# The first batch's quantisation spread over twenty items of cross attention and shared with GpSimd, its rows sent ahead of the down weights, and the first projections' waits split

## The reference

```python
x = layernorm(x + self_attention(x, W_K, W_Q, W_V, W_O))   # 16 heads of 128, causal
x = layernorm(x + gamma * cross_attention(x, ctx, ctx))    # 8 heads of 64, no projections
x = layernorm(x + ffn(x))

def ffn(x):                                    # hidden 2048
    xhat = (x - mean(x)) / sqrt(var(x) + 1e-8)
    s = 127 / max(abs(xhat))                   # for each token
    xq = clip(round(s * xhat), -128, 127) / s
    g = silu(xq @ sign(W_g).T)
    u = xq @ sign(W_u).T
    return (g * u) @ sign(W_d).T
```

## Time and profile before

| | us |
|---|---|
| median of 3 runs (lowest, highest) | 1461.12 (1459.65, 1461.98) |
| the profiled execution's own time | 1461.33 |
| its span, first to last instruction | 1459.5 |
| self attention, about | 0 to 985 |
| cross attention, about | 985 to 1212 |
| ffn, about | 1212 to 1459.5 |

### The profile page before, as it was taken

One profiled execution on the slowest core, in us unless ns is written; L12 is line 12 of the kernel. 1 busy time (PEld: TensorE's weight loads), 2 busy tenths in 40 slices (PEclk: granted clock), 3 DMA queues, 4 the chain that ended last, 5 costly groups with the idle time before them and its releaser, 6 DMA issues.

```text
span 1459.5 us, 23316 instructions
## 1 busy us (share of the span) xinstructions
PE 1416.3 (97%) x6912; PEld 1137.0 (78%) x6912; DVE 1086.8 (74%) x2346; ACT 713.3 (49%) x1528; POOL 624.9 (43%) x499
## 2 busy tenths in 40 slices
PE   7999999999999999999999999988999998999998
PEld 6788888888888888888888888867887774655665
DVE  4667676777777776767677777689989996698846
ACT  3444535354444444454545444547887873333333
POOL 1334434334253443443534425355655653344434
PEclk9999999999999999999999999999999999999999
DMA  6566666666666666666666666665556642101101
GB/s 182 150 181 180 190 162 181 169 185 177 174 174 184 167 175 180 180 190 162 185 175 180 179 175 183 197 171 151 131 142 164 185 124 95 37 1 65 37 29 58
DMA packets 210606, 219.33 MB, mean 150 GB/s; under 512 B 99712, under 2 KB 177536, under 8 KB 210560
## 3 DMA queue, kind: packets, MB, share of 16 engines
q1 hardware_dynamic: 209408, 218.24, 53.4%
q10 hardware_dynamic: 1152, 0.52, 0.2%
HBM read 128.98 MB, written 81.85 MB: 144 GB/s over the span
## 4 chain that ended last, share of the span: by engine, by line
PE 83%; DVE 9%; DMA 4%; ACT 2%; issue 1%; SPq 1%; POOL 1%; ACTq 0%; POOLq 0%; DVEq 0%
PE bank L517 35%; PE bank L555 11%; PE bank L524 8%; PE bank L542 8%; PE bank L1642 7%; PE bank L1630 6%; PE bank L1199 3%; PE bank L1153 2%; PE bank L1168 2%; DVE xneg_max L1303 1%; DVE xpT_lo L1310 1%; DMA xs<-rows_pair 1%; ACT xprobs L1241 1%; DVE acc L851 1%; DMA turned_scratch<-turned 1%
## 5 line engine op out<-in xcount | busy, mean ns | idle before, releaser
L662 ACT ACTIVATE probs<-probs,neg_max 128x128 f32<-128x128 f32 (+3 forms) x256 | 142.8, 559 | 356.9 <-DVE neg_max L791 349.6
L473 POOL TENSOR_TENSOR v_lo<-placed,v_hi 128x512 fp32r<-128x512 f32 x63 | 81.7, 1297 | 349.9 <-ACT v_hi L668 349.9
L475 POOL TENSOR_TENSOR pT_lo<-placed,pT_hi 128x1280 fp32r<-128x1280 f32 x63 | 186.3, 2957 | 0.0
L851 DVE SCALAR_TENSOR_TENSOR acc<-bank,prob_recip,acc 128x512 f32<-128x512 f32 x256 | 174.5, 745 | 4.9
L1598 POOL TENSOR_TENSOR prod_lo<-prod,prod_hi 128x512 fp32r<-128x512 f32 x64 | 85.1, 1329 | 137.3 <-ACT prod_hi L1680 137.3
L1092 POOL TENSOR_SCALAR xprobs<-xprobs,xprob_recip 128x512 f32<-128x512 f32 x128 | 87.3, 700 | 90.8 <-DVE xprob_recip L1314 90.8
L791 DVE CUSTOM_DVE_ANT_0 probs<-bank,mask 128x128 f32<-128x128 f32 (+3 forms) x256 | 117.2, 480 | 8.4
L766 DVE TENSOR_TENSOR qT_lo<-bank,qT_hi 128x512 fp32r<-128x512 f32 x64 | 44.2, 690 | 104.7 <-ACT qT_hi L650 104.7
L803 DVE STREAM_TRANSPOSE turned<-probs 128x256 f32<-128x256 f32 (+1 forms) x384 | 113.8, 361 | 0.0
L1642 PE MATMUL bank<-wdT_f32r,prod_hi 128*128 128x512 f32 x256 | 111.6, 436 | 0.8 <-POOL prod_lo L1598 0.6
L1241 ACT ACTIVATE xprobs<-bank,xneg_max 128x512 f32<-128x512 f32 x128 | 89.2, 697 | 42.3 <-DVE xneg_max L1303 40.6
(11 more groups left out here) (156 smaller groups left out, 3816.3 us busy)
## 6 DMA issues: line engine op xcount, KB each, us to landing
turned_scratch<-turned SPq DMA_DIRECT2D x64, 896.0 KB, 3.8
placed<-turned_scratch SPq DMA_DIRECT2D x252, 224.0 KB, 4.1
cp<-context_halves SPq DMA_DIRECT2D x64, 256.0 KB, 3.9
context_halves<-ctx_halves SPq DMA_DIRECT2D x16, 512.0 KB, 4.7
xs<-rows_pair SPq DMA_DIRECT2D x60, 128.0 KB, 3.7
acc<-in_x_dram SPq DMA_DIRECT2D x16, 256.0 KB, 4.4
rows<-in_L_attn_W_V_dram SPq DMA_DIRECT2D x64, 64.0 KB, 2.2
rows<-in_L_attn_W_O_dram SPq DMA_DIRECT2D x64, 64.0 KB, 2.7
```

The source lines that it names most:

```text
L475: nc.gpsimd.tensor_tensor(pT[par][1][:], landed_probs(landing), pT[par][0][:].bitcast(F32), ALU.subtract).then_inc(p_lo, 1)
L662: nc.scalar.activation(probs[:, cols], probs[:, cols], ACT.Exp, bias=low[:, par, t:t + 1], scale=-1.0, accum_out=total[:, par, t:t + 1]).t ...
L851: nc.vector.scalar_tensor_tensor(out=acc[:, b * NT + t, :], in0=s_bank[t][:], scalar=recip[:, b, t:t + 1], in1=acc[:, b * NT + t, :], op0= ...
```

## The change

Four things are edited. (1) In the first projections (batch 0) TensorE waits ahead of each of the three passes for what that pass reads, instead of ahead of the first for all; ScalarE copies wk after x3's cast, and VectorE turns wk ahead of x2 and wq after x3. (2) The quantisation of batch 0 runs beside items 9 to 28 of cross attention. VectorE keeps the statistics, the variances, the maxima, the steps and the turning. (3) Both norms' application and scaling with rounding become two GpSimd instructions for each of four tiles, with a wait between the two; they stand at the end of GpSimd's list of items 11 to 14, 17 to 20 and 23 to 26, the powers at the end of items 10 and 16. (4) SP sends and lands the turned rows ahead of all down weights, and `row_step` ahead of `xqT`.

```diff
...
         cross.begin_gpsimd(pool)
     def tensor(pe):
-        def project(name, b, bank, full):
+        def project(name, b, bank, full, first=False):
             w = wT[name]
             n = 0
             for wp, xp in SPLIT:
+                if first:
+                    pe.wait_ge((w_lo if wp else w_hi)[name], 1)
+                    pe.wait_ge(xt_lo if xp else xt_hi, NT)
                 for c in range(NC):
                     n += 1
                     last = nc.tensor.matmul(bank[:], w[wp][:, c * P:(c + 1) * P], xT[xp][:, c, b * S:(b + 1) * S],
...
                 scores()
             else:
                 full, free, bank = {"k": (k_full, k_lo, k_bank), "q": (q_full, q_lo, q_bank), "v": (v_full, v_turn, v_bank)}[what]
-                if n == 0:
-                    pe.wait_ge(w_lo["w" + what], 1)
-                else:
+                if n > 0:
                     pe.wait_ge(free, n)
-                pe.wait_ge(xt_lo, (n + 1) * NT)
-                project("w" + what, n, bank, full)
+                    pe.wait_ge(xt_lo, (n + 1) * NT)
+                project("w" + what, n, bank, full, n == 0)
         def step(h, b):
             i = h * B + b
...
         for name in BEGIN:
             what, n = name[0], int(name[1:])
             if what == "x":
-                if n == 2:
-                    weight_hi("wk", 1)
                 act.wait_ge(xt_full, n + 1)
                 nc.scalar.copy(xT[0][:, :, n * P:(n + 1) * P],
                                X_BANK[n][:].rearrange("p (c n) -> p c n", n=P)).then_inc(xt_hi, 1)
                 if n == 3:
+                    weight_hi("wk", 1)
                     weight_hi("wq", 1)
                 if n == 4:
                     weight_hi("wv", 1)
...
         for name in BEGIN:
             what, n = name[0], int(name[1:])
             if what == "x":
-                if n == 1:
+                if n == 2:
                     turn_weight("wk", 1)
-                if n == 3:
-                    turn_weight("wq", 1)
                 if n == 4:
                     turn_weight("wv", 1)
                 if n == 8:
...
                 cols = slice(n * P, (n + 1) * P)
                 nc.vector.tensor_tensor(xT[1][:, :, cols], X_BANK[n][:].rearrange("p (c n) -> p c n", n=P),
                                         xT[0][:, :, cols].bitcast(F32), ALU.subtract).then_inc(xt_lo, 1)
+                if n == 3:
+                    turn_weight("wq", 1)
             elif what == "k":
                 lo(kT, k_bank, k_hi, n + 1, k_lo)
             elif what == "q":
...
         return b + (h + d) // XH, (h + d) % XH
-    QUANT_FROM = B - 2
-    GAP = 2 * NT + 1
-    NQ_AT, AMAX_AT = GAP + NT, 2 * (GAP + NT)
-    LEVELS_AT = AMAX_AT + NT
-    SCALE_AT = LEVELS_AT + 1
-    ROUND_AT, TURN_AT = SCALE_AT + NT, SCALE_AT + 2 * NT
+    QUANT_FROM = XH + 1
+    N2_POW, N2_APPLY, NQ_STATS, NQ_POW, NQ_APPLY, AMAX, ROUNDED, TURN = 1, 2, 4, 7, 8, 10, 14, 18
     def exists(n, limit):
...
         pool.wait_ge(norm1.rstd_ready, 2)
     def gpsimd(pool):
+        def quantise_beside(pool, i):
+
+            if i == N2_POW:
+                norm_gpsimd(nc, pool, quant.norm2, k.minus_half, 0)
+            if 0 <= i - N2_APPLY < NT:
+                quant.apply_beside(pool, quant.norm2, quant.normed, 0, i - N2_APPLY)
+            if i == NQ_POW:
+                norm_gpsimd(nc, pool, quant.norm_q, k.minus_half, 0)
+            if 0 <= i - NQ_APPLY < NT:
+                quant.apply_beside(pool, quant.norm_q, quant.hat, 1, i - NQ_APPLY)
+            if 0 <= i - ROUNDED < NT:
+                quant.round_beside(pool, i - ROUNDED)
+
         def step(b, h):
             m = b * XH + h
             if h % 2 == 0 and exists(m + 4, ITEMS):
...
                 queries_lo(pool, nb, nh // 2)
             if is_item(b, h, 1, 1):
                 quant.clear_steps(pool)
-            if is_item(b, h, QUANT_FROM, 2):
-                norm_gpsimd(nc, pool, quant.norm2, k.minus_half, 0)
-            if is_item(b, h, QUANT_FROM, 6):
-                norm_gpsimd(nc, pool, quant.norm_q, k.minus_half, 0)
             if exists(m + 2, ITEMS):
                 normalise(pool, m + 2, (h + 2) % 4)
             if pair_ends(b, h):
...
             if normalises(b) and h == XH - 1:
                 norm_gpsimd(nc, pool, norm1, k.minus_half, b + 2)
                 pool.wait_ge(norm1.rstd_ready, b + 3)
+            quantise_beside(pool, m - QUANT_FROM)
         batches(pool, step)
...
                     norm1_stats(dve, b + 2, NORM1_STATS.index(u))
                 if u == NORM1_VAR:
                     norm_var(nc, dve, k, norm1, LN_EPS, b + 2)
-                return
-            v = (b - QUANT_FROM) * XH * NT + u
-            if v % NT == 2:
-                return
-            n = v // NT * (NT - 1) + min(v % NT, 2)
-            if n == 0:
+            quantise_beside(dve, b * XH + u // NT - QUANT_FROM, u % NT)
+
+        def quantise_beside(dve, i, j):
+
+            if i == 0 and j == 0:
                 dve.wait_ge(z_added, PAIRS + 1)
                 dve.wait_ge(signs.kept, H * 48 + 1)
                 dve.wait_ge(source.halves_kept, H * 16)
-            quantise_beside(dve, n)
-
-        def quantise_beside(dve, n):
-
-            for norm, at, eps, stage in ((quant.norm2, 0, LN_EPS, quant.normed), (quant.norm_q, NQ_AT, FFN_EPS, quant.hat)):
-                if 0 <= n - at < NT:
-                    quant.stats(dve, norm, 0, n - at)
-                if n - at == NT:
-                    norm_var(nc, dve, k, norm, eps, 0)
-                if 0 <= n - at - GAP < NT:
-                    quant.apply(dve, norm, stage, 0, n - at - GAP)
-            if 0 <= n - AMAX_AT < NT:
-                quant.tile_amax(dve, 0, n - AMAX_AT)
-            if n == LEVELS_AT:
+            if i == 0:
+                quant.stats(dve, quant.norm2, 0, j)
+            if i == N2_POW and j == 0:
+                norm_var(nc, dve, k, quant.norm2, LN_EPS, 0)
+            if 0 <= i - NQ_STATS < NT and j == 0:
+                quant.wait_beside(dve, quant.norm2.done, 0, i - NQ_STATS)
+                stats_tile(nc, dve, quant.norm_q, tile_of(0, i - NQ_STATS), i - NQ_STATS, 0)
+            if i == NQ_POW and j == 1:
+                norm_var(nc, dve, k, quant.norm_q, FFN_EPS, 0)
+            if 0 <= i - AMAX < NT and j == 0:
+                quant.wait_beside(dve, quant.norm_q.done, 1, i - AMAX)
+                quant.tile_amax(dve, 0, i - AMAX)
+            if i == AMAX + NT - 1 and j == 1:
                 quant.levels(dve, 0)
-            if 0 <= n - SCALE_AT < NT:
-                quant.scale_tile(dve, 0, n - SCALE_AT)
-            if 0 <= n - ROUND_AT < NT:
-                quant.round_tile(dve, 0, n - ROUND_AT)
-            if n == TURN_AT:
+            if 0 <= i - TURN < 2 and j % 2 == 1:
+                quant.turn_tile(dve, 0, 2 * (i - TURN) + j // 2)
+            if i == TURN and j == 0:
                 quant.turn_steps(dve, 0)
-            if 0 <= n - TURN_AT < NT:
-                quant.turn_tile(dve, 0, n - TURN_AT)
         def step(b, h):
             m = b * XH + h
...
         self.x_scratch = nc.dram_tensor("x_turned_scratch", (P, self.E, NC * NT * self.R), BF16).ap()
         self.step_scratch = nc.dram_tensor("steps_scratch", (P, self.R), F32).ap()
         self.cleared = sem("steps_cleared")
+        self.beside_half, self.beside_done = sem("quant_half_done"), sem("quant_tile_done")
         self.amax_ready, self.recip_done, self.per_unit_ready = sem("amax_ready"), sem("amax_recip_done"), sem("per_unit_ready")
         self.scaled_ready, self.xq_ready = sem("scaled_ready"), sem("xq_ready")
         self.x_turn, self.step_turn = sem("xq_turned"), sem("steps_turn_done")
...
     def apply(self, dve, norm, out, b, t):
         apply_tile(self.nc, dve, norm, self.normed(b, t), out(b, t), t, b)
+    def wait_beside(self, dve, done, stage, t):
+
+        if t == NT - 1:
+            dve.wait_ge(done, 1)
+        else:
+            dve.wait_ge(self.beside_done, stage * (NT - 1) + t + 1)
+
+    def apply_beside(self, pool, norm, out, stage, t):
+
+        x = out(0, t)
+        if t == 0:
+            pool.wait_ge(norm.rstd_ready, 1)
+        self.nc.gpsimd.tensor_scalar(x, self.normed(0, t), norm.mv[:, t, 0:1], 1.0, ALU.subtract, ALU.mult).then_inc(self.beside_half, 1)
+        pool.wait_ge(self.beside_half, stage * NT + t + 1)
+        self.nc.gpsimd.tensor_scalar(x, x, norm.rstd[:, t:t + 1], 1.0, ALU.mult, ALU.mult
+                                     ).then_inc(norm.done if t == NT - 1 else self.beside_done, 1)
+
+    def round_beside(self, pool, t):
+
+        if t == 0:
+            pool.wait_ge(self.per_unit_ready, 1)
+        self.nc.gpsimd.tensor_scalar(self.scaled[:, t, :], self.xhat[:, t, :], self.per_unit[:, t:t + 1], ROUND,
+                                     ALU.mult, ALU.add).then_inc(self.beside_half, 1)
+        pool.wait_ge(self.beside_half, 2 * NT + t + 1)
```

(18 more changed lines are left out.)

## The result

The changed kernel took 1450.73 us (median of 6 runs, 1450.15 to 1452.37) where the kernel before took 1460.89 on the same chip: ratio 0.9934, 95% interval 0.9921 to 0.9947, or 9.6 us less (7.7 to 11.5). On another chip it took 1449.78 beside 1461.06: ratio 0.9916 (0.9902 to 0.993), 12.3 us less. It is faster, by two thirds to four fifths of the 15.1 us of the forecast.

The account below looks back on a forecast made before the run. TensorE, busy in 97% of the span, was taken as the bound, with gains where it waits or VectorE bounds cross attention. -5.1 - 3.7 - 6.3 = -15.1 from 1461.1 gave 1446.0 us, range 1441 to 1452.5.

Parts of the forecast that it names:

- edit 1: First projections: k0 starts at 9.8 instead of 12.58 and runs at full clock; -5.1 us, bounds 2.8 and 6.7.
- items 9 to 15: Cross attention: added statistics and a variance fill VectorE; +1.5 us, bounds nothing and 3.
- items 16 to 23: Cross attention: VectorE sheds statistics and applications, gains maxima and steps; 55.6 us instead of 57.73, -2.1.
- items 24 to 28: Cross attention: VectorE sheds quantisation work and gains four turned tiles; 33.6 us instead of 36.28, -2.7.
- end of cross attention: The turning no longer stands at the end of cross attention; -0.4 us, bounds 0 and 1.
- edit 4 with the early quantisation: Start of the ffn: rows and steps arrive in time, the gate waits for TensorE alone; -6.3 us.
- the price of a GpSimd tile: Quantisation in cross attention: 0.7 us an instruction, 1.45 a tile with the wait; instruction bounds 0.7 and 1.3.
- rival D: Start of the ffn: rows arrive late and hold the gate by 3 us; 1449 us, chance 5%.
- C: Cross attention: six GpSimd tiles ahead of `queries_lo` cost 0.8 to 1.3 us each; 1449 to 1452 us, 15%.
- E: Cross attention, slower: GpSimd's tile takes 2.8 us and is on the path, costing 17 us; 1466.7 us, 3%.
- slack of 1.4 us ahead of `queries_lo`: Cross attention: margin before scores wait for xs, just used up by a 1.45 us tile; 0.25 us counted each, 1.5 in all.
- rival B: First projections: the clock falls in the first gap all the same, k0 at half, 2.3 us lost; 1448.3 us, 22%.

Follow-up runs that it names:

- c0: The changed kernel run again, unaltered, on another chip: 1449.78 us, ratio 0.9916 to the kernel before.
- e2: The kernel before with only SP's new order (turned rows ahead of down weights, `row_step` ahead of `xqT`), quantisation where it was: 1463.73 us, ratio 1.0013.
- e4: The changed kernel with GpSimd's two subtractions written as additions of the negated operand: 1447.5 us, ratio 0.9904 to the kernel before.
- e6: e4 with the rounding's minimum with 127 replaced by a multiplication with 1.0, so without the clip: 1446.91 us, ratio 0.9908 to the kernel before.
- e5: The changed kernel with twelve unused transposes of the identity on TensorE at the start, eight ahead of x0 and four ahead of k0: 1450.15 us, ratio 0.9923.
- e8: The changed kernel with the first projections' new waits and order undone, the rest kept: 1453.83 us, ratio 0.995 to the kernel before.
- e1: The kernel before with only the first projections' split waits and new ScalarE and VectorE order: 1456.89 us, ratio 0.997.
- e9: e6 with 24 unused transposes on TensorE ahead of each of self attention's last two output products: 1449.06 us, ratio 0.9925 to the kernel before.
- e10: e9 with the second set cut to 18 transposes and placed behind the first of VectorE's four additions: 1446.15 us, ratio 0.9891 to the kernel before.

## Why the prediction was right, and where it was off

| step | forecast | measured |
|---|---|---|
| edit 1 | -5.1 (-2.8 to -6.7) | -4.4 alone (-6.1 to -2.6) |
| items 9 to 15 | +1.5 (0 to +3) | +1.9, c0 +2.0 |
| items 16 to 23 | -2.1 | -2.0, c0 -1.5 |
| items 24 to 28 | -2.7 | -2.1, c0 -2.0 |
| end of cross attention | -0.4 | -0.6 |
| edit 4 with the early quantisation | -6.3 | -6.3 |
| sum; measured: the medians of the whole | -15.1 | -9.6 and -12.3 |

The measured time lies in the range that was stated, 4.7 us above the forecast of 1446.0. Edit 4 and the order of the stretches of cross attention came as forecast; the price of a GpSimd tile, the state of the clock at k0 and the handover did not.

**Edit 4** came out as summed, 2.24 for 2.3 us from the last product to the gate, and the gate waits for TensorE alone; rival D is out. Two of its durations were off and offset each other. The write was taken at 5.3 us and took 2.6. `xqT` was given no duration of its own: issued until 1200.6 and at most 7.1 us in landing, it was there by 1207.7, 1.6 us before `gate_up` wanted it at 1209.27. That this is near the "microsecond or more" of the prediction is luck. (The write near 1185 does not follow from the prediction's own terms either: T(29) + 0.6 would be 1189.6, and it was 1196.08, 1.1 after T(29).)

Why `xqT` took 5.7 to 7.1 us, and 2.6 to 2.9 before, is seen in batch 1, where no down weights are issued near it. DMA issues from 1240 to 1275 us in the kernel before, then in the changed one:

```profile
xqT<-x_turned_scratch SPq DMA_DIRECT2D x4, 128.0 KB, 2.8
```

```profile
xqT<-x_turned_scratch SPq DMA_DIRECT2D x4, 128.0 KB, 4.9
```

What differs there is that `row_step` is issued ahead of `xqT` instead of behind it: 2.1 us (batch 3: 5.1 for 2.8). The remaining 1.5 us, up to the median of 6.4 in batch 0, go with the 16 down transfers. So the half of edit 4 that moved `row_step` forward has a price that the prediction left out, and the spare time hid it. An order with `xqT` first and the down weights last was not run. In e2, where the rows are written 12.5 us later (1208.58 for 1196.08), TensorE and the gate wait for `xqT`, and the order by itself gains nothing. The prediction put the gain down to edit 4; it needs the early quantisation as well. The early quantisation without edit 4 was not run, but SP issues the twelve down transfers ahead of the rows until 1206.15 in the kernel before, so the rows could hardly have left sooner.

**Cross attention** was forecast at -3.7 and came to -3.0 and -2.2. The sign and place of each stretch were right, item 10 standing in for item 9 as the one near 8 us. The failing step is the price of a GpSimd tile: "I take 0.7" for an instruction, 1.45 a tile, from the nearest row, the division with its multiplication. It is 2.6 to 2.7, and with it one of the prediction's signs of being wrong, a tile of over 2 us, did appear. The engine and the shape were the same, the operations (subtract, minimum) were not, and the bound of 1.3 from two-input work did not hold them either. e4 and e6 price the two in cross attention: 0.9 us for the subtraction (weak, as said) and 2.3 for the minimum, 3.2 together, which four traces on either side show (211.3 to 211.7 against 214.1 to 215.1). The minimum's part ends in the step where VectorE "may wait a microsecond with room behind it": it waits 2.46 us in item 27, and that item takes 8.3 us instead of 6.4. With both gone cross attention takes 5.3 to 5.8 us less than before, more than the forecast. That GpSimd's work would slow VectorE's tiles of norm 1 does not show: the eight from 1050 to 1161 us take 0.65 us each, before 0.68.

The Trainium skill ("GPSIMD Engine Reference", Engine selection) puts GpSimd at about line rate with one input. The rows roughly agree for multiplication and addition (0.69, where VectorE takes 0.52 to 0.58) and do not for the subtraction (2.0) or a minimum (1.92).

**Rivals C and E** named the engine but not the place. E was to decide from 2.4 us a tile, and the tile costs 2.7; yet scores wait for xs only once, for 0.4 us, and that is at 990.98, before T(0) (who waited for the tile xs, 985 to 1212 us):

```profile
who waited for it (us, times):
  DVE xneg_max L1309: 5.0, 19
  PE bank L1159: 0.4, 1
```

The slack of 1.4 us ahead of `queries_lo`, worked from one item and the latest landings, was taken too small. What the slow tile costs came at the list's other end, at the rows that VectorE turns.

**Edit 1** started k0 as forecast (9.38 for 9.8; before 12.58). What k0 costs came out in part. Over the eleven profiled executions with edit 1, k0 took 3.02 or 3.03 in five, 4.4 or 4.5 in two, 5.1 to 5.5 in four. The forecast and rival B argued whether the clock falls in the gap ahead of k0, and both took for granted that TensorE enters that gap at full clock. In the change it does not: the sixteen transposes of x0 to x3 are slow already,

```profile
3.94 4.25 PE L574 MATMUL bank<-ident,acc 128*128 128x128 f32 x16 [3.94 <-DMA acc<-in_x_dram]
```

each beginning 0.21 us after the one before it within a tile, where later ones follow at 0.12. Each trace records when TensorE first rises from half to full clock, and the spacing of its matmuls shrinks at that moment. It lies between 7.2 and 8.1 us, just before or among x3's transposes, in the five with a full k0, at 12.7 in two and between 14.5 and 15.4 in four, e5 among them. The gap of 1.2 to 1.3 us, which the forecast said would not make it fall, did not in any of the five that had risen; B's fall happened in none of the eleven, though its cost came in four of them for another reason. Without edit 1 k0 was at half in all three executions: in e2 and e8 TensorE had not risen yet, and before it rose at 7.3 (x3's four transposes took 0.75 us there, in c0 1.12) and fell at 10.7, inside its wait of 4.3 us. So edit 1 gives k0 its full clock when the rise comes early, and when it comes is not in the kernel's hand as far as these runs show.

The Trainium skill says in "TensorE: Matmul & The Clock Gate" (What's actually happening) that the activity window behind the clock does not start with the kernel, so that the moment of the rise varies by 0.5 us to either side. That it differs between executions agrees; its spread does not, 7.2 to 15.4 us here.

The bound of 6.7 us, with the later fall gone too, was also reached. The first output product starts 2.6 to 2.9 us earlier than before in the four executions with a slow k0, 5.2 in two, and 6.5 to 6.9 in the five with a full k0. In the four the clock falls again at 45.2 to 46.2 us (before, at 48.3); in the other seven it does not. Windows of the change and of e1, the same stretch of work:

```profile
43.20:48.90 5.70, 3.49 (x14) 3.04 (x15) 4.93 (x12) 3.37 (x7) 3.33 (x2) 0.76 0.10 40
```

```profile
40.60:46.30 5.70, 3.47 (x19) 3.06 (x20) 4.90 (x12) 3.30 (x7) 3.35 (x2) 1.00 0.09 40
```

That fall costs 1.2 us, for which the bound had 1.6. Why it stays away when the first rise comes by 12.7 us is open. The mean of the eleven is 5.0 us, near the 5.1 of the forecast, but as a mixture of three cases and not as the one case that was summed; part of it is lost again in the handover. What is measured for the whole kernel is e1's 4.4 us.

**The handover** is what the sum left out. It held all between k0 and T(0) fixed ("and so does self attention, which TensorE bounds"). The last output product ran at full clock in the execution that was profiled before and in e5, at half in eight others, in part in two; at half T(0) comes 15.4 to 16.0 us after its start, at full (e9 and e10 too) 13.3 to 13.6. So the profile of before was some 2.2 us lucky there. Whether edit 1 makes the fall more frequent is open: e2 and e8, without edit 1, fell too, and how often plain executions of the kernel before do cannot be read from times.

So 2.8 to 5.5 us are missing against 15.1. In the traces 0.7 to 1.5 of them lie in cross attention, where GpSimd's price (3.2 by e4 and e6) covers them more than once, and none in edit 4. The rest is not settled: edit 1 alone (e1) is 0.7 short, and the other edits (e8, 7.3) are 1.3 short of the 2.2 and 6.3 that its trace shows in cross attention and at the gate, both within their intervals. The change's two comparisons differ by 2.7, and its two profiled executions were the slowest of their runs (1452.37 of 1450.15 to 1452.37, 1452.1 of 1446.49 to 1452.1). The clock at k0, near 46 us and in the handover moves single executions by as much; that it makes up the rest is argued from single traces, not shown by medians.
